# A Mamba scan with a quantised MLP in 125 hand-ordered slots: the order of each engine's steps inside a slot changed, and TensorE given products of zeros

## What is computed

```python
# cross part: a selective scan over the context, 512 channels, 16 states
x1 = silu(causal_conv4(in_proj(ctx)) + conv_b)               # u
dt_low, B, C = split(x_proj @ x1)
dt = softplus(dt_proj @ dt_low + dt_proj_b)
state = state * exp(dt * A) + (dt * u) * B                   # per step t, 16 states
y = (state * C).sum(n) + D * u
x = x + tanh(g_xattn) * y * silu(layernorm(x))
# MLP with 8-bit activations and ternary weights
xn = rmsnorm(layernorm(x)); h = silu(q(xn) @ w1q) * (q(xn) @ w2q)
x = x + tanh(g_ffn) * (q(rmsnorm(h)) @ w3q)
```

## Time and profile before

| | |
|---|---|
| median of 3 runs | 708.96 us |
| the profiled execution | 708.85 us, its span (first to last instruction) 707.1 us |
| busy: POOL, VectorE, ScalarE, TensorE | 602.3, 598.6, 523.3, 513.7 us |
| mean granted TensorE clock | 0.891 of full |

### The profile page before, as it was taken

One profiled execution on the slowest core, in us unless ns is written; L12 is line 12 of the kernel. 1 busy time (PEld: TensorE's weight loads), 2 busy tenths in 40 slices (PEclk: granted clock), 3 DMA queues, 4 the chain that ended last, 5 costly groups with the idle time before them and its releaser, 6 DMA issues.

```text
span 707.1 us, 8143 instructions
## 1 busy us (share of the span) xinstructions
PE 513.7 (73%) x2562; PEld 315.4 (45%) x2562; DVE 598.6 (85%) x842; ACT 523.3 (74%) x980; POOL 602.3 (85%) x295
## 2 busy tenths in 40 slices
PE   9787889883446639777566577677686777758897
PEld 3243444433443426454544345355453544445554
DVE  7679768877997998989958998998889989888865
ACT  5754867599987647868686787798798797677654
POOL 1499899999999959799998999898998999888421
PEclk9899999998567969899685889899999999989999
DMA  5696875499910000146400000035520000000001
GB/s 171 217 403 218 309 297 191 152 331 405 357 61 6 30 1 15 60 161 211 165 20 1 30 0 16 1 132 211 193 76 1 15 2 16 0 15 17 1 16 45
DMA packets 23930, 80.78 MB, mean 114 GB/s; under 512 B 2432, under 2 KB 4608, under 8 KB 20816
## 3 DMA queue, kind: packets, MB, share of 16 engines
q1 hardware_dynamic: 23888, 80.27, 30.9%
HBM read 72.53 MB, written 7.73 MB: 114 GB/s over the span
## 4 chain that ended last, share of the span: by engine, by line
DVE 30%; ACT 27%; PE 20%; issue 11%; POOL 7%; DMA 3%; SPq 1%; DVEq 0%; ACTq 0%
DVE hh L767 8%; ACT da L730 7%; DVE hh L764 4%; POOL hh L812 3%; PE bank_t L1138 3%; POOL hh L704 3%; PE bank_y L845 3%; PE bank_b L1000 3%; PE bank_a L994 3%; DMA wq<-x 2%; DVE sm L1060 2%; ACT room L1035 2%; ACT room L1149 2%; ACT room L1014 2%; ACT da L737 2%
## 5 line engine op out<-in xcount | busy, mean ns | idle before, releaser
L767 DVE TENSOR_TENSOR_SCAN hh<-da,hh 128x1024 f32<-128x1024 f32 x91 | 206.5, 2279 | 10.7 <-POOL hh L704 6.7
L845 PE MATMUL bank_y<-ident,hh 128*128 128x128 f32 x1024 | 147.3, 294 | 20.4 <-POOL hh L812 16.2
L845 PEld LDWEIGHTS bank_y<-ident,hh 128*128 128x128 f32 x1024 | 131.4, 154 | 51.6 <-POOL hh L812 25.5
L807 POOL TENSOR_TENSOR hh<-hh,cc 128x1024 f32<-128x1024 f32 x62 | 146.1, 2357 | 4.0 <-ACT hl L749 2.9
L812 POOL TENSOR_TENSOR hh<-hh,cc 128x1024 f32<-128x1024 f32 x61 | 143.6, 2354 | 0.0
L704 POOL TENSOR_TENSOR hh<-pair,bb 128x1024 f32<-128x1024 f32 x30 | 70.7, 2358 | 26.7 <-DMA bb<-xd_scratch 24.9
L698 POOL TENSOR_TENSOR hh<-wq,bb 128x1024 f32<-128x1024 f32 x32 | 75.3, 2354 | 12.4 <-PE bank_y L845 12.4
L704 POOL TENSOR_TENSOR hh<-wq,bb 128x1024 f32<-128x1024 f32 x32 | 75.3, 2352 | 11.9 <-PE bank_y L845 11.7
L764 DVE TENSOR_TENSOR_SCAN hh<-da,hl,hh 128x256 f32<-128x256 f32 x128 | 85.2, 729 | 0.0
L698 POOL TENSOR_TENSOR hh<-pair,bb 128x1024 f32<-128x1024 f32 x32 | 75.4, 2357 | 9.1 <-PE bank_y L845 9.1
L730 ACT ACTIVATE da<-wq,cst 128x256 f32<-128x256 f32 x128 | 53.3, 466 | 12.8 <-DVE hh L764 12.7
(11 more groups left out here) (256 smaller groups left out, 1042.3 us busy)
## 6 DMA issues: line engine op xcount, KB each, us to landing
bb<-xd_scratch SPq DMA_DIRECT2D x32, 512.0 KB, 5.1
cc<-xd_scratch SPq DMA_DIRECT2D x32, 512.0 KB, 6.8
wq<-weights SPq DMA_DIRECT2D x12, 1024.0 KB, 6.7
stage<-weights SPq DMA_DIRECT2D x8, 1024.0 KB, 6.1
xin<-x SPq DMA_DIRECT2D x4, 1024.0 KB, 5.2
room<-weights SPq DMA_DIRECT2D x4, 1024.0 KB, 8.5
u_scratch<-wq SPq DMA_DIRECT2D x6, 512.0 KB, 3.1
wq<-x SPq DMA_DIRECT2D x2, 1024.0 KB, 18.2
```

The lines of the kernel that those rows point to most:

```text
L767: ins = v.tensor_tensor_scan(to, da, h, 0.0, ALU.mult, ALU.add)
L807: ins = g_.tensor_tensor(quarters(flat(hh[k % NH])), quarters(flat(hh[k % NH])), cc[:, n:n + 4, t], ALU.mult)
L845: mm = pe.matmul(bank_y[:, (first + c) * P:(first + c + 1) * P], flat(hh[k % NH])[:, at:at + P], ident[:, :], start=False, stop=(s == STEP ...
```

## The change

- **Orders.** In every engine's loop over the slots the steps of a slot stand in another order. TensorE: `ab_tensor` is split into `a_tensor` and `b_tensor`; in a slot with both, `ht(0)`, `a`, `ht(1)`, `b` follow one another eight slots after a tile's start, where `ht(0)`, `ht(1)`, `a`, `b` did; nine slots after it the order stays `ht(2)`, `ht(3)`, `a`, `b`. ScalarE copies `ht(0)` and `ht(2)` before the squares, `ht(1)` at the end of its slot. POOL does `times_c` before the small powers. VectorE begins with the second part of the scales and ends with z.
- **Slots.** `center_scalar` and `stats_vector` come one slot later, `PAIR[2]` is 26 for 25, `PAIR[5]` 65 for 66 (and SyncE's load of batch 3's dt rows, which follows it, one slot earlier), z of tile 15 is 117 for 116, two roundings 32 and 35 for 31 and 34; five roundings go to ScalarE for four. `c_by_vector` is (14, 45, 53, 63, 77).
- **The gate** of tile 4 is done like the others, and `gate_late` is gone.
- **Products of zeros.** `fill` multiplies 80 columns of zeros with `ident` and adds to 128 columns of `bank_y`. Skipped where the slot number is a multiple of 8, they are 12 in the four slots of `FILL` and 104 in 33 of the 36 slots of `FILL_LATE` (32, 72 and 96 are skipped); six more stand before the first slot. That is 122 products.
- **The end.** Small exchanges in TensorE's and ScalarE's lists for tiles 12 and 13.

The core of the diff:

```diff
-PAIR = {2: 25, 3: 37, 4: 49, 5: 66, 6: 87, 7: 99}
+PAIR = {2: 26, 3: 37, 4: 49, 5: 65, 6: 87, 7: 99}
+FILL = {114: 3, 115: 3, 116: 3, 117: 3}
+FILL_LATE = {4: 3, 5: 3, 7: 3, 10: 1, 17: 1, 19: 3, 21: 3, 22: 5, 31: 5, 32: 5, 42: 5, 47: 1, 50: 2, 71: 3, 72: 3, 73: 3, 74: 6, 77: 2, 84: 2, 85: 2, 86: 2, 87: 2, 89: 3, 90: 3, 96: 1, 99: 2, 100: 3, 101: 3, 102: 2, 109: 2, 110: 5, 111: 5, 113: 5, 114: 5, 115: 3, 116: 6}
+FILL_FIRST = (0, 0, 6)
...
+BY_VECTOR = (14, 45, 53, 63, 77)
 def c_by_vector(k):
-    return k % STEPS == 5 and 40 < k < 80
+    return k in BY_VECTOR
...
+        def fill(pe, n):
+            for _ in range(n):
+                pe.matmul(bank_y[0:80, 0:P], zeros[:, :], ident[:, :], start=False, stop=False, skip_group_check=True)
...
-            if g == NE:
-                YV.did(v.tensor_tensor(gbuf[:, q, :], bank_y[:, :], gbuf[:, q, :], ALU.mult), ("y", g))
-                return
...
-        def gate_late(v, g):
-            v.wait_ge(*WA.of(("sign", NW - 1)))
-            v.wait_ge(*YV.of(("y", g)))
-            YV.did(v.tensor_tensor(columns(x2[1], 0), by_rows(gbuf[:, 0, :]), columns(xin, 0), ALU.add))
...
         def rounded_by_scalar(i):
-            return i in (1, 4, 7, 10)
+            return i in (0, 3, 7, 9, 10)
...
POOL
                 for k in range(SLOTS):
+                    if k < ALL and not c_by_vector(k):
+                        times_c(g_, k)
+                    for i in range(END):
+                        if k == tile_slot(i) + 7:
+                            rh_pool(g_, i)
                     if k == 10:
                         g_.wait_ge(*ZA.of("var"))
...
ScalarE
                     for first, n, done in TURNS:
-                        if k == done + 2:
+                        if k == done + 3:
                             center_scalar(act, first, n)
...
+                    for i in range(END - 1):
+                        if k == tile_slot(i) + 8:
+                            hqt_scalar(act, i, 0)
...
+                    for i in range(END - 1):
+                        if k == tile_slot(i) + 9:
+                            hqt_scalar(act, i, 2)
+                    for i in range(END):
+                        c = k - tile_slot(i) - 1
                         if 0 <= c < NCH:
                             square_scalar(act, i, c)
...
+                    for i in range(END - 1):
+                        if k == tile_slot(i) + 9:
                             hqt_scalar(act, i, 3)
...
+                    for i in range(END - 1):
+                        if k == tile_slot(i) + 8:
+                            hqt_scalar(act, i, 1)
...
TensorE
+                    if k % STEPS:
+                        fill(pe, FILL.get(k, 0))
...
+                    if k % STEPS:
+                        fill(pe, FILL_LATE.get(k, 0))
+                    for i in range(END - 1):
+                        if k == tile_slot(i) + 9:
+                            ht_tensor(pe, i, 2)
+                    for i in range(END - 1):
+                        if k == tile_slot(i) + 8:
+                            ht_tensor(pe, i, 0)
+                    for i in range(END - 1):
+                        if k == tile_slot(i) + 9:
+                            ht_tensor(pe, i, 3)
                     for i in range(END + 1):
                         c = k - tile_slot(i)
                         if 0 <= c < NCH:
-                            ab_tensor(pe, i, c)
-                        if k == turned(i):
-                            ht_tensor(pe, i, 0)
+                            a_tensor(pe, i, c)
+                    for i in range(END - 1):
+                        if k == tile_slot(i) + 8:
                             ht_tensor(pe, i, 1)
-                        if k == turned(i) + 1:
-                            ht_tensor(pe, i, 2)
-                            ht_tensor(pe, i, 3)
+                    for i in range(END + 1):
+                        c = k - tile_slot(i)
+                        if 0 <= c < NCH:
+                            b_tensor(pe, i, c)
...
VectorE
                     for first, n, done in TURNS:
-                        if k == done + 1:
+                        if k == done + 2:
                             for i in range(first, first + n):
                                 stats_vector(v, i)
...
-                    if k == PER + 3 * NE:
-                        gate_late(v, NE)
```

More of the change, by code:

```diff
@@ L358, in warm, with fill_first @@
                 pe.matmul(bank[:, :], spare[:, 0:P], spare[:, :], start=True, stop=True)
+        def fill(pe, n):
+            for _ in range(n):
+                pe.matmul(bank_y[0:80, 0:P], zeros[:, :], ident[:, :], start=False, stop=False, skip_group_check=True)
+        def fill_first(pe, n):
+            for _ in range(n):
+                pe.matmul(bank_y[0:80, 0:P], zeros[:, :], ident[:, :], start=True, stop=True)
         def first_front_scalar(act):
@@ L1355, in _ @@
                             cfac_pool(g_, first, n)
[L1356 to L1360, removed]
                     if k + LEAD < ALL:
@@ L1397, in _ @@
                 for k in range(SLOTS):
+                    for i in range(NW):
+                        if k == round_slot(i) and rounded_by_scalar(i):
+                            weight_round_scalar(act, i)
                     for i in range(END):
@@ L1515, in _ @@
                     spread_tensor(pe, n)
-                for g in range(1, NE):
-                    dt_proj(pe, g)
+                dt_proj(pe, 1)
+                pe.wait_ge(*BV.of(1))
+                fill_first(pe, FILL_FIRST[0])
+                dt_proj(pe, 2)
+                fill_first(pe, FILL_FIRST[1])
+                dt_proj(pe, 3)
+                fill_first(pe, FILL_FIRST[2])
                 for k in range(SLOTS):
@@ L1520, in _ @@
                         sums(pe, k - 1)
-                    for b in (1, 2, 3):
-                        front_tensor(pe, b, k)
+                    for i in range(END + 1):
+                        if k == tile_slot(i) - 1:
+                            xt_tensor(pe, i)
                     for n in PAIR:
@@ L1624, in _ @@
                     for i in range(END):
+                        if k == tile_slot(i) + 7:
+                            scales_vector(v, i, 1)
+                    for i in range(END):
                         c = k - tile_slot(i) - 1
@@ L1642, in _ @@
                             row_statistics(v, i)
+                    for i in range(END):
+                        if k == tile_slot(i) + 5:
+                            scales_vector(v, i, 0)
                     for n in PAIR:
@@ L1659, in _ @@
                                 aggr_vector(v, i)
-                        if k == done + 4:
-                            rows_vector(v, first, n)
+                    for i in range(END - 1):
+                        if k == tile_slot(i) + 10:
+                            out_vector(v, i)
+                    for i in range(NE):
+                        if k == z_turn_slot(i):
+                            y_first(v, i)
+                    if k + LEAD - 1 < ALL and c_by_vector(k + LEAD - 1):
+                        times_c_vector(v, k + LEAD - 1)
+                    for i in range(END):
+                        if k == tile_slot(i) + 4:
+                            peak_vector(v, i, 1)
+                    for i in range(1, NW, 2):
+                        if k == sum_slot(i):
+                            weight_sum_vector(v, i)
+                    for i in range(END):
+                        if k == tile_slot(i) + 2:
+                            peak_vector(v, i, 0)
                     for i in TILES:
```

131 lines of the change are left out of this document (62 added, 69 removed).

## The result

The changed kernel takes 676.88 us, the median of 4 runs (675.80 to 678.67), against 709.21 us for the kernel before on the same chip: a ratio of 0.9546, interval 0.9515 to 0.9577.

A forecast was written before the change was run, and what follows sets the result against it. POOL, waiting 42.9 us in its stretch, mostly for TensorE's `sums`, was taken as the bound, VectorE second. Terms -7.5 - 1.9 - 2.9 - 13 - 3 + 8 = -20.3 took 708.85 to 688.5 us; range 675 to 704.

The forecast's parts named there:

- The frame: Whole kernel: head 27.65, POOL stretch 633.8, tail 45.6 us; only POOL's 42.9 us of waits in the stretch can go.
- case (a): Whole kernel: the change works as forecast, 682 to 696 us; chance 50%.
- The gate: Tile 4's gate: adding straight from `bank_y` removes the blocked 8.21 us VectorE addition and POOL's 7.51 us loss; -7.5 us.
- POOL's small power: Slot 10: `times_c(10)` placed ahead covers POOL's 1.88 us wait for ScalarE's variance; -1.9 us.
- Centring and softplus apart: Slot 66: softplus moves to 65, centring to 67, so POOL's 2.91 us wait for the kept state goes; -2.9 us.
- The transposes: Six POOL waits, 18.1 us together: `a` fills TensorE's wait for ScalarE's copy, clock holds; net 2.2 each, -13 us.
- The clock's half of that: After TensorE's waits at the transposes: if the clock holds, `a`, `b` and `sums` get back 1.75 us a place.
- Rival (c): At the transposes: the clock falls despite the zeros, giving 2.6 us for 13; 699 us, chance 8%.
- The other waits for sums: POOL's 14 smaller waits for `sums`, 9.4 us: a third goes; -3 us.
- new waits: All engines, orders changed: waits the trace can't show yet, between 0 and 18 us; +8 us.
- VectorE's limit: VectorE as second bound: 433 us of work at 93% busy needs 466 us, limiting the time to 675 us.
- Rival (d): Whole kernel: nearly all waits go and VectorE's 675 us binds; 670 to 681 us, chance 13%.

## Why the prediction was right, and which steps were not

- **The frame** held: head and tail kept their lengths, and POOL's waits, 42.9 us, were what could go. 32 of them went. Of the signs, POOL's stretch came to 601.6 us for 613 and its waits for the sums to 7.9 us for 10 to 15; the granted clock of 0.92 stayed short of 0.93. The time is in the range, but outside the 682 to 696 us of case (a), which had half the chances. And the 0.5% by which a run was to tell a difference is too little for the kernel before, whose 39 executions lie between 698.6 and 710.4 us.
- **The gate**, -7.5: the run of it alone gives -8.5. Right in mechanism and size, with one correction: the addition isn't always starved (1.38 us where it was put back), and 10 of 39 executions of the kernel before are as fast as if it were not. For those the term would be nothing, if the short addition is their cause.
- **POOL's small power**, -1.9: no wait of POOL is left at slot 10. Not run by itself.
- **Centring and softplus apart**, -2.9: undoing it costs 4.2 us. The step named the place at slot 66; the run shows the largest new wait behind TensorE's slot 37 and the rest in other waits for the sums. Size near, place wrong.
- **The transposes**, -13: the sum is near the 10.8 us of that order on its own, but its make-up is partly luck. The order is worth 26.7 us when taken out last, for the 0.87 us at each place that I worked out: I priced only `a` moved into the wait, and put the copies ahead of the squares at nothing. I also counted six places as alike. Slot 101 has no transposes (`a` waited 3.81 us for VectorE there) and slot 85 has `ht(2)` and `ht(3)`, whose order did not change; the wait of slot 85 was still 3.18 us with the transposes moved.
- **The clock's half of that**, 6 x 1.75 = 10.5 us, was right in that the lower clock costs `a`, `b` and `sums` up to 1.75 us and that POOL pays it where TensorE is late (1.70 for 1.70 us in slot 121). It was wrong in what keeps the clock up: the moved transposes do, at slots 90, 101, 114 and 120, without a single product of zeros. Where TensorE isn't late, as in slot 85 of the changed kernel, the lower clock costs nothing (0.17 us of POOL's time with the products of zeros). Rival (c) named the mechanism of the products: the clock falls all the same, at five of six places on the old order, and two of the six slots, 52 and 120, hold none of them. Its time of 699 us was wrong, as it gave the order only 0.87 us a place.
- **The products of zeros**: no cost in idle time, as forecast; the 6 x 0.44 us charged to the transposes were not paid, either.
- **The other waits for sums**, -3, and **new waits**, +8: the first was too small, the second too large. All waits of POOL together are 11 us after, so of the 9.4 us of small waits little is left, and the new one of weight is 2.82 us. The +8 is the larger part of the 11.6 us by which the forecast lies above the measured time.
- **VectorE's limit**, 675 us at 93%: the measured 92% and 676.9 us stand at it. Rival (d), at 13%, gives the measured time, 670 to 681 us, with three quarters of the waits gone. That VectorE is what binds there is not shown: it was not made faster.

## What to carry to other kernels

Where one engine paces a kernel through a ring of buffers, add up its waits between its first and last instruction: that sum is the most that reordering inside this stretch can give. Look then for the pair of engines that hand one small bank to and fro, put independent work into the gap on one side, and on the other move the copy ahead of whatever nobody waits for; do both: TensorE's order undone alone cost 9.4 us, both undone 26.7 us. The copies' place alone was not run. A lower clock is worth looking at only where the engine is late already, and there the moved steps held it up where added products mostly did not. An elementwise VectorE step with both inputs in SBUF should read one of them from PSUM where POOL never pauses.

## What was not expected of the hardware

A VectorE step of 8 columns with two SBUF inputs lasted 5.85, 10.21, 0.14 and 1.79 us in turn; for the 0.14 POOL had just been idle, beside the others it had no gap. The two long ones ended when a POOL instruction did, the 10.21 us one only when POOL had run dry. The gate's addition of 512 columns took 8.21 us in the kernel before, and 1.38 put back into the changed kernel. With one SBUF input, 8 columns took 0.85 to 2.18 us and ended with the POOL instruction under way. The granted clock rose from 0.90 to 0.92 with 16.5 us of added products of zeros, and the time stayed. In slot 121 the lower clock made the sums 1.70 us later and POOL's wait 1.70 us longer; in slot 85 of the changed kernel without products of zeros it cost POOL nothing.
